# Windowed attention with a quantized matmul on eight cores: how block 0 loads and uses its key and query weights

## The reference, cut to what matters

```
xn  = layernorm(x)                                   # x: 32 x 2048 x 1024, f32
q, k, v = split(xn @ w_in.T)                         # 16 heads of 64
    # blocks of 512 tokens; a query sees the keys 0 to 512 positions back,
    # those of its own block and of the block before it
    s   = q @ k.T / 8 + slope[h] * (qpos - kpos)
    o   = softmax(s) @ v
attn = o @ w_out.T
    # quantized matmul, one scale for each row
    xs  = max(rowmax|xn|, 1e-6) / 127
    xq  = clip(round(xn / xs), -128, 127)
ffn  = (xq @ weight_q.T) * xs * weight_scale + bias
out  = x + attn + ffn
```

## Time and profile before

| | us |
|---|---|
| median of 3 runs | 1654.83 |
| the runs | 1652.48 to 1738.67 |
| the profiled execution, device time | 1654.68 |
| its slowest core (core 2), span from first to last instruction | 1653.1 |
| its fastest core (core 5), span | 1645.1 |

### The profile page before, as it was taken

The page is one execution under the profiler, slowest core; times in us unless marked ns, Lnnn a source line. Parts: engine busy times, 40 slices in busy tenths (PEclk is TensorE's granted clock), DMA queues, the critical chain, the costliest instruction groups (busy, mean ns, idle before and its releaser), DMA issues.

```text
span 1653.1 us, 29485 instructions; the slowest of 8 cores (1645.1 to 1653.1 us)
## 1 busy us (share of the span) xinstructions
PE 1566.1 (95%) x8568; PEld 749.9 (45%) x8736; DVE 939.6 (57%) x1696; ACT 1060.1 (64%) x2093; POOL 840.0 (51%) x1242
## 2 busy tenths in 40 slices
PE   4859999999999999999999999999999999999998
PEld 2325444454444445444444544445444444544443
DVE  4535646556475655746566564655647566564454
ACT  3546676766746667776665677667775566767662
POOL 5324536445473644536455563645537554563365
PEclk9979999999999999999999999999999999999999
DMA  7784453433545344353445434344354634435232
GB/s 161 185 222 116 124 147 107 128 116 122 147 133 151 115 128 121 113 146 114 128 132 149 142 109 136 113 121 135 109 141 127 173 116 115 141 109 147 78 79 82
DMA packets 208707, 213.98 MB, mean 129 GB/s; under 512 B 139932, under 2 KB 140060, under 8 KB 208040
## 3 DMA queue, kind: packets, MB, share of 16 engines
q1 hardware_dynamic: 205672, 201.60, 42.2%
q0 software_dynamic: 2880, 10.49, 3.5%
HBM read 149.12 MB, written 37.75 MB: 113 GB/s over the span
## 4 chain that ended last, share of the span: by engine, by line
PE 85%; ACT 6%; DMA 4%; issue 3%; DVE 1%; POOL 1%; SPq 0%; ACTq 0%; DVEq 0%; POOLq 0%
PE dn L578 61%; PE ob L822 7%; PE oa L822 7%; PE sc L730 5%; PE sc L753 5%; ACT p L770 4%; DMA wqk<-w 1%; DMA w2bf<-wqk 1%; ACT r L837 1%; ACT r L835 1%; DMA xpre<-x 1%; SPq L160 0%; DVE p L806 0%; POOL xn L462 0%; DMA xnfm<-xn 0%
## 5 line engine op out<-in xcount | busy, mean ns | idle before, releaser
L770 ACT ACTIVATE p<-sc,kbias_sb 128x512 bf16<-128x512 f32 (+3 forms) x1120 | 489.9, 536 | 235.8 <-PE sc L753 158.6
L578 PE MATMUL dn<-xnfm,wqk 128*128 128x512 bf16 x1996 | 477.1, 382 | 14.6 <-DMA xnfm<-xn 9.6
L664 POOL TENSOR_TENSOR u<-u,xres 128x256 f32<-128x256 f32 x240 | 169.9, 729 | 337.8 <-DVE u L681 337.5
L806 DVE TENSOR_TENSOR p<-p,tri_sb 128x512 bf16<-128x512 bf16 (+1 forms) x608 | 251.3, 414 | 146.4 <-ACT p L787 112.5
L578 PEld LDWEIGHTS dn<-xnfm,wqk 128*128 128x128 bf16 x2048 | 192.6, 98 | 244.5 <-issue 34.4
L787 ACT ACTIVATE p<-sc 128x1024 bf16<-128x1024 f32 (+3 forms) x228 | 214.9, 954 | 107.8 <-PE sc L730 105.9
L578 PE MATMUL dn<-wq_sb,xqfm 128*128 128x512 bf16 x1003 | 240.5, 381 | 6.0 <-DMA xqfm<-xq 2.8
L578 PE MATMUL dn<-wout_sb,ofm 128*128 128x512 bf16 x984 | 233.0, 379 | 6.5 <-issue 4.0
L578 PE MATMUL dn<-wv_sb,xnfm 128*128 128x512 bf16 x985 | 237.2, 380 | 2.0
L822 PE MATMUL oa<-p,vst 128*128 128x512 bf16 (+3 forms) x888 | 217.4, 300 | 4.6 <-DVE ofm L848 4.4
L822 PE MATMUL ob<-p,vst 128*128 128x256 bf16 (+3 forms) x896 | 218.7, 300 | 0.4
(11 more groups left out here) (61 smaller groups left out, 1634.4 us busy)
## 6 DMA issues: line engine op xcount, KB each, us to landing
wqk<-w2bf SPq DMA_DIRECT2D x240, 256.0 KB, 3.0
xpre<-x SPq DMA_DIRECT2D x64, 512.0 KB, 4.5
xres<-x SPq DMA_DIRECT2D x64, 512.0 KB, 4.5
out<-u SPq DMA_DIRECT2D x124, 256.0 KB, 2.2
wqk<-w POOLq DMA_DIRECT2D x16, 256.0 KB, 8.7
w2bf<-wqk SPq DMA_DIRECT2D x16, 256.0 KB, 5.5
wv_sb<-wv POOLq DMA_DIRECT2D x2, 1024.0 KB, 11.8
wq_sb<-wq POOLq DMA_DIRECT2D x1, 2048.0 KB, 13.8
```

The lines of the kernel that those rows point to most:

```text
L578: tok = P.op("tensor", lambda e, k=k: e.matmul(out=dn[b][:, :], lhsT=lhs(k), rhs=rhs(k), start=(k == 0), stop=(k == n - 1)), waits=(waits ...
L664: a = P.op("gpsimd", lambda e, q=q: e.tensor_tensor(out=u[:, 256 * q:256 * q + 256], in0=u[:, 256 * q:256 * q + 256], in1=buf[:, 512 * hal ...
L770: tok = P.op("scalar", lambda e, c0=c0, c1=c1, hp=hp, o=o: e.activation(out=pbuf[b % NPB][:, 512 * hp + c0:512 * hp + c1], in_=sc[b % 2][: ...
L806: mask_done[b] = P.op("vector", lambda e: e.tensor_tensor(out=pt, in0=pt, in1=m, op=ALU.mult), waits=[exp_done[b], c_tok])
```

## The change

**Block 0's K and Q weights get a place of their own.** Tiles 0 to 7 are loaded into `wq_sb` and 8 to 15 into `wout_sb`, which nothing else uses until block 1. They don't wait for buffers, and nothing is written to the scratch in block 0. `wq` and `wout` are loaded over them later, `wq` at `(3, 1)` and `wout` at `(6, 1)` of block 0, each once the last group that reads the old tiles is done.

**Block 1 loads the f32 weights once more**, through the `wqk` buffers and POOL, and the scratch copies are made there (`store_wqk`, two groups ahead of use). The scratch is read from block 2 on. Tiles 16 to 19 are issued at `(1, 0)` of block 0.

**Block 0's rows are scaled by ACT** (`xn_first`): `xn = x * rstd - mean * rstd` in one instruction from the loaded rows. POOL makes only the small columns. The mean subtraction in place, row maximum and scales of block 0 come later: the first on POOL before block 0's attention (`FIRST_MEAN`), the other two on DVE in slot 0 and at `(1, 0)` of block 0. The turns stand at `(1, 1)` to `(1, 4)` of the round before block 0, where they stood at `(6, 0)` to `(6, 3)`.

**Another order of first loads.** The first two weight tiles wait for the first rows of `x`; the others, and both halves of `wv`, follow between the tiles. Block 1's rows are loaded, normalized and measured at places of their own (`SECOND_*`).

```diff
-XN_TURN = {(6, 0): 0, (6, 1): 1, (6, 2): 2, (6, 3): 3}
-FIRST_STAT = {(1, 0): 0, (1, 1): 1, (1, 2): 2, (1, 3): 3}
-FIRST_AMAX = {(2, 0): 0, (2, 1): 1, (2, 2): 2, (2, 3): 3}
+FIRST_NORM = {(1, 0): 0, (1, 1): 1, (1, 2): 2, (1, 3): 3}
+FIRST_TURN = {(1, 1): 0, (1, 2): 1, (1, 3): 2, (1, 4): 3}
+FIRST_WEIGHTS = {(1, 0): (2, 3), (2, 4): (8, 9, 10, 11, 12, 13, 14, 15)}
+FIRST_MEAN = {(2, 0): 0, (2, 1): 1, (2, 2): 2, (2, 3): 3}
+FIRST_AMAX = {(0, 1): 0, (0, 2): 1, (0, 3): 2, (0, 4): 3}
+FIRST_SCALES = (1, 0)
+SECOND_LOAD = {(0, 3): 0, (0, 4): 1, (2, 3): 2, (3, 0): 3}
+SECOND_STAT = {(1, 4): 0, (2, 1): 1, (3, 3): 2, (4, 1): 3}
...
+        def wtile(seq):
+            if seq < 16:
+                t_ = wq_sb if seq < 8 else wout_sb
+                return t_[:, 1024 * (seq % 8):1024 * (seq % 8) + 1024]
+            return wqk[seq % 4][:, :]
+        def load_first(seq, waits=()):
+            wqk_ready[seq] = P.dma("gpsimd", wtile(seq), w2h[fc_of(seq)], f"WB{seq}", waits=waits)
         def load_wqk(seq):
-            if seq >= 16 * NT:
+            if not 16 <= seq < 16 * NT:
                 return
             i = seq % 4
-            if seq < 16:
-                waits = wqk_free[i] + ([w2bf_done[seq - 4]] if seq >= 4 else [])
+            if seq < 32:
+                waits = wqk_free[i] + ([w2bf_done[seq - 4]] if seq >= 20 else [])
                 wqk_ready[seq] = P.dma("gpsimd", wqk[i][:, :], w2h[fc_of(seq)], f"WG{i}", waits=waits)
-                w2bf_done[seq] = P.dma("sync", w2bf[fc_of(seq)], wqk[i][:, :], f"WS{i}",
-                                       waits=[wqk_ready[seq]])
...
+        def store_wqk(seq):
+            if 16 <= seq < 32:
+                w2bf_done[seq] = P.dma("sync", w2bf[fc_of(seq)], wqk[seq % 4][:, :], f"WS{seq % 4}",
+                                       waits=[wqk_ready[seq]])
...
-        for seq in range(4):
-            i = seq
-            wqk_ready[seq] = P.dma("gpsimd", wqk[i][:, :], w2h[fc_of(seq)], f"WG{i}")
+        for seq in range(2):
+            load_first(seq, [xpre_ready[(0, 0)]])
...
+        def load_wq():
+            late_w["wq"] = P.dma("gpsimd", wq_sb[:, :], wqh, "WQ", waits=wb_free[0])
+        def load_wout():
+            late_w["wout"] = P.dma("gpsimd", wout_sb[:, :], wouth, "WO", waits=wb_free[1])
...
+        def xn_first(tc):
+            x = xsrc(0, tc)
+            P.op("vector", lambda e: e.bn_stats(out=stbn[tc][:, 0:6], in_=x[:, 0:512]),
+                 waits=[xpre_ready[(0, tc)]], inc=False)
...
+            m = P.op("gpsimd", lambda e: e.tensor_tensor(
+                out=nmr[:, tc:tc + 1], in0=negm[0][:, tc:tc + 1], in1=rstd[0][:, tc:tc + 1], op=ALU.mult),
+                waits=[n, r])
...
+            xn_ready[(0, tc)] = P.op("scalar", lambda e: e.activation(
+                out=xn[tc][:, :], in_=x[:, :], func=AF.Identity, bias=nmr[:, tc:tc + 1],
+                scale=rstd[0][:, tc:tc + 1]), waits=[m])
...
-            load_wqk(seq + 4)
+            store_wqk(seq + 2)
+            if seq + 4 >= 32:
+                load_wqk(seq + 4)
             def evac():
+                if 20 <= seq + 4 < 32:
+                    load_wqk(seq + 4)
...
-                    if t == -1 and at == (7, 0):
-                        load_late_weights()
-                    if t == 0 and at == (4, 0):
-                        load_late_weights2()
+                    if t == 0 and at == (3, 1):
+                        load_wq()
+                    if t == 0 and at == (6, 1):
+                        load_wout()
```

More of the change, by code:

```diff
@@ L236, in build_nc @@
         ubuf = [sb(f"u{i}", [128, 512], F32) for i in range(4)]
-        small = sb("small", [128, 122], F32)
+        small = sb("small", [128, 126], F32)
         small_at = 0
@@ L265, in build_nc @@
         dma_sems = (["TN", "TQ0", "TQ1", "C", "CK", "CI", "CW", "CB", "XS2", "XS3", "WV0", "WV1", "WO", "WQ", "EA", "EB", "FA", "FB"]
[L266 removed]
+                    + [f"W{i}" for i in range(4)] + [f"WB{i}" for i in range(16)] + [f"WG{i}" for i in range(4)] + [f"WS{i}" for i in range(4)]
                     + [f"XP{i}" for i in range(2)] + [f"XR{i}" for i in range(NXR)]
@@ L418, in set_ones, with load_wv1 @@
             ones_tok.append(P.op("gpsimd", lambda e: e.memset(vones, 1.0)))
-        def load_late_weights():
+        def load_wv1():
             wv_tok.append(P.dma("gpsimd", wv_sb[:, 4096:8192], wvh[1], "WV1"))
[L423 to L429, removed]
+        def load_wq():
+            late_w["wq"] = P.dma("gpsimd", wq_sb[:, :], wqh, "WQ", waits=wb_free[0])
+        def load_wout():
+            late_w["wout"] = P.dma("gpsimd", wout_sb[:, :], wouth, "WO", waits=wb_free[1])
         def xn_load(t, tc):
@@ L913, in build_nc @@
                             den_plan[base + 7] = (tp, pp, tok)
[L915 to L921, removed]
+                    if t + 1 == 0:
+                        if at in FIRST_NORM:
+                            xn_first(FIRST_NORM[at])
+                        if at == (1, 1):
+                            load_wv0()
+                        if at == (1, 4):
+                            for seq in (4, 5):
+                                load_first(seq)
+                            load_wv1()
+                            for seq in (6, 7):
+                                load_first(seq)
+                            set_ones()
+                        elif at in FIRST_WEIGHTS:
+                            for seq in FIRST_WEIGHTS[at]:
+                                load_first(seq)
+                        if at in FIRST_MEAN:
+                            xn_less_mean(FIRST_MEAN[at])
+                    elif t + 1 < NT:
+                        load, stat, norm_at, amax, scales_at = (
+                            (SECOND_LOAD, SECOND_STAT, SECOND_NORM, SECOND_AMAX, XN_SCALES) if t == 0
+                            else (XN_LOAD, XN_STAT, XN_NORM, XN_AMAX, XN_SCALES))
+                        if t == 0 and at in FIRST_AMAX:
+                            xn_amax(0, FIRST_AMAX[at])
+                        if t == 0 and at == FIRST_SCALES:
+                            xn_scales(0)
+                        if at in load:
+                            xn_load(t + 1, load[at])
+                        if at in stat:
+                            xn_stat(t + 1, stat[at])
                         if at in norm_at:
                             xn_norm(t + 1, norm_at[at])
-                        if at in amax_at:
-                            xn_amax(t + 1, amax_at[at])
-                        if at == XN_SCALES:
+                        if at in amax:
+                            xn_amax(t + 1, amax[at])
+                        if at == scales_at:
                             xn_scales(t + 1)
```

46 lines of the change are left out of this document (35 added, 11 removed).

## The result

The changed kernel takes 1646.62 us (median of 6 runs, from 1646.16 up), the kernel before 1656.78 on the same chip. In some runs (two of these six before, one of six after) the cores of half the chip show a lower clock and the time is longer: the ratio and its interval leave such runs out, the medians in this text are over all runs (without them 1654.3 and 1646.5). The ratio is 0.995, 95% interval 0.9933 to 0.9967. So it is 5.5 to 11 us faster, some 8 at the middle, where the forecast was 13.8. The profiled execution took 1646.16 us; its slowest core, 5, has a span of 1644.6.

What follows compares the result with a forecast made beforehand. PE bounds the kernel, and the start of block 1 sets the span. After 13.2 us gained by Q7's end and the transposes' wait beside `wout`, block 1 starts 13.8 us earlier: 1654.7 - 13.8 = 1641, range 1629 to 1648.

Steps and rivals of the forecast that it cites:

- The path: PE's timeline up to block 1's first score matmul; that start sets the span one for one, with 1524 us behind it.
- the mechanism: Between Q7 and K+0: `wout`'s 16 KB packets, turn by turn with the transposes' small ones, all but stop them.
- the term for the transposes: Ahead of K+0: transposes wait beside `wout`, which ends near 99.6, then take 3 more us; K+0 at 102.6, gain 13.8.
- The start: Up to the first matmul of K0: it starts at 20.2 (18.5 to 22.0), a gain of 7.15 us.
- Inside block 0: Up to Q7's end: waits of 0.55, 2.22 and 1.59 us go, and 1.7 us of low clock.
- no wait of PE on `norm` over 1 us in block 0: Sign to look for in the changed kernel's profile: PE waits at most 1 us for DVE's `norm` in block 0.
- Block 1: Takes over 16 f32 loads and scratch copies at no cost; tile 20 issued near 106, landing at 119, wanted at 122.
- A: Rival, between Q7 and K+0: transposes get their share or `wout` starts too late; gain 23.9 us, 1631; chance 0.20.
- B: Rival, ahead of Q7: late weights or a returning DVE wait lose half of 13.2 us; 1648 (1645 to 1655); chance 0.13.
- C: Rival, in block 1: loads and scratch copies overrun their two slots, costing 36 us; 1677; chance 0.04.

Runs made afterwards that it cites:

- experiment 9: Changed kernel with tiles 0 to 7 in `wout_sb`, 8 to 15 in `wq_sb`, `wout` loaded at (3, 3), `wq` after the transposes: 1633.06 us, ratio 0.9869.
- 11: Against experiment 9: statistics of x(1, 2) and x(1, 3) one beat later, `wout` loaded at (3, 4): 1634.52 us, ratio 0.9875.
- experiment 1: Changed kernel, but the load of `wout` also waits for the last transpose of block 1: 1636.97 us, ratio 0.9896.
- experiment 10: Against experiment 9: statistics of x(1, 2) and x(1, 3) one beat later, `wout` still at (3, 3): 1641.88 us, ratio 0.9919.
- experiment 2: Changed kernel with `wout` loaded in eight pieces of 128x1024, 2 KB packets instead of 16 KB: 1646.75 us, ratio 0.9959.

## Which step of the prediction failed, and what it had right

The path, the direction and the mechanism were right. The size was not: a gain of 13.8 us was forecast and some 8 came, 1641 against 1646.6. The step that failed is the term for the transposes, in the sentence "`wout` starts to move some 3 us after its issue [...] so it ends near 84.1 + 3 + 12.5 = 99.6". On core 2 `wout` took 17.3 us from issue to landing and not 15.5, and from the end of Q7 to K+0 it was 21.0 us and not 18.6. Each step on that core, from which the forecast was worked out:

| | forecast | measured |
|---|---|---|
| K0 | 20.2 | 20.8 |
| end of Q7 | 84.0 | 85.5 |
| `wout` landed | 99.6 | 103.3 |
| K+0 | 102.6 | 106.5 |
| block 1 | 115.4 | 119.6 |
| block 1 to the end | 1524 | 1524.3 |

- **The start**: 0.6 late here, 1.6 on core 5. There the rows landed at 7.76 and not at 6.6, POOL's columns began at 9.65 and not at 8.4, and ACT's scaling pass was 1.24 us and not 1.01. No weight was late: PE waits for none in block 0.
- **Inside block 0**: the waits of 0.55, 2.22 and 1.59 went, as did the low clock behind them. I did not see the new one of 1.15 us at (3, 3), though the order of DVE's instructions shows it: statistics stand there between `norm` and the CAST. With the 0.6 of the start it makes up the 1.5 at the end of Q7. The sign "no wait of PE on `norm` over 1 us in block 0" does not hold as I wrote it: the 3.06 us in slot 7 are in both kernels. The sum had them, inside its 9.6 us from Q7 to K+0.
- **The transposes**: `wout` was issued at 86.0, 1.9 later than I had it, of which Q7 explains 1.5. It then took 17.3 us and not 15.5. The 12.5 was the time that `wout` added behind `wq`, next to other traffic. Next to the transposes it took 16.3 to 18.9 over the eight cores, and 14.9 with the engines almost to itself (experiment 9). From its landing to K+0 it was 3.1 us, as forecast.
- **Which core is last**: I took core 2's gain. It was 9.6 (129.13 to 119.56), but core 3 starts block 1 last now, at 120.81. Before, the cores spread over 8 us, after over 3.6. The last core gains 8.3.
- **Block 1**: took the loads and copies at no cost: 1523.3 to 1524.7 us from its start on, over the eight cores. The dates that I gave for it were off: tile 20 was issued at 111.5 on core 5 and not near 106, and landed in 4.1 us and not 12.9 (and by the forecast's own start of block 1, 115.4 and not 114.8, it was wanted at 122.6). The two errors cancelled, which was luck.
- **The rivals**: A (no contention, 1631) was wrong for this kernel; experiment 9 takes the contention away and measures 1633, so its price of 23.9 us was about right. What makes the 2 us between them is not shown: the start was 1 us later than forecast there (21.2 in the mean), and 11, without the wait at 71 us, gained nothing. B and C did not occur. The time alone could not tell the forecast from B, whose 1645 to 1655 hold 1646.6 while the forecast's own bounds, 1637 to 1646, just miss it; Q7 ending at 85.5 and the wait of 11 us behind it tell them apart.

The 5.4 us by which the last core starts block 1 late (120.8 and not 115.4) are then 0.6 of the start, 0.9 more up to the end of Q7, 0.4 to the issue of `wout`, 1.8 in its duration, 0.1 to K+0, 0.3 to block 1, and 1.25 between core 2 and core 3.

What stays open: why `wout` takes 16 to 19 us beside the transposes when these get under 2% of the DMA time (its packets take longer there, see the last section, but not why), and what part of the 6 us that core 7 loses in block 1 of experiment 1 is due to which transfer.

## What to carry to other kernels

When a wait ends, look at what else was queued on the same event: here the removal of a scratch copy let the transposes and a 4 MB load start on the end of one matmul, and the load took back 10 to 13 us. A large load from the converting queue belongs where no short transfer is waited for, and one can see such a hole in the DMA row of the profile (here 76 to 84 us); a single wait, or a place two beats later, moved the time by 8 to 10 us, as much as the whole change. And if a load's time of issue rests on another wait of its engine, as in experiment 10, state it as a wait of its own before moving anything.

## What the runs showed of the hardware

- While both have work, two DMA queues mostly take turns packet by packet, whatever the packets hold: 39 and 38 with 256 bytes against 16 KB, 365 and 366 with 2 KB, 41 and 40 with row loads beside `wout`. An exception stands in experiment 2 (59 against 187). The Trainium skill, "DMA: Bandwidth & Descriptors" under "Queues, rings and completion order", says that an engine goes round its queues by packets. The trace agrees, but for that exception. It adds that a packet holds several descriptors as a rule; for the transposes no such bundle is seen, as they passed one record of some 256 bytes a turn.
- What a packet of a converting load costs the others went with what it reads (share x 16 engines x time / packets): 0.55 us for a row of 16 KB from int8, 1.4 from f32 beside the row loads and with the engines to itself (0.995 x 64 / 46 in experiment 9, 76 to 80 us), and 1.5 to 1.8 from f32 beside the transposes (0.967 x 64 / 41 and 1.089 x 64 / 38).
- The issuing engine is stopped too: SP was in the issue of the four transposes for 19.36 us, 14.00 of them in one piece, where 5.87 is enough in experiment 9.
